# Second attention of a two-layer decoder: 384 equal slots, values in two blocks a group, transfers by four heads, norm rows on ScalarE

## The reference

```python
h = layernorm(x)                                   # over 256 columns
q, k, v from h @ W_kqv + b_kqv                     # 16 heads of 16
att = q @ k.T / sqrt(16) + slope * (j - i)         # j > i masked
x = x + (softmax(att) @ v) @ W_proj + b_proj
```

## Time and profile before

| | us |
|---|---|
| median of 3 runs | 2440.0 |
| the runs | 2440.0, 2426.59, 2440.98 |
| the profiled execution, span from first to last instruction | 2440.0 |
| the stage's first projection to its last addition | 808 to 1405 |
| first key score to last | 844.3 to 1390.6 |

### The profile page before, as it was taken

One profiled execution on the slowest core, in us unless ns is written; L12 is line 12 of the kernel. 1 busy time (PEld: TensorE's weight loads), 2 busy tenths in 40 slices (PEclk: granted clock), 3 DMA queues, 4 the chain that ended last, 5 costly groups with the idle time before them and its releaser, 6 DMA issues. The chain is left out here.

```text
span 2440.0 us, 41800 instructions
## 1 busy us (share of the span) xinstructions
PE 2194.9 (90%) x13788; PEld 1746.8 (72%) x13789; DVE 1186.6 (49%) x3470; ACT 961.3 (39%) x1878; POOL 641.1 (26%) x821
## 2 busy tenths in 40 slices
PE   6997888779999688888889879988999999999998
PEld 4664455568999445555555457778899999999998
DVE  4553788755334456666665345535322222222245
ACT  2222455333444344444444413320255555555411
POOL 1112667744401233333332211105400000000063
PEclk9997999889999789998999889989999999999999
DMA  9930000123222424442333010054211111111033
GB/s 321 386 109 1 1 1 33 46 72 117 70 69 84 97 54 88 88 88 49 83 80 70 2 56 4 3 193 148 88 31 34 34 34 34 32 32 34 26 110 101
DMA packets 151007, 183.45 MB, mean 75 GB/s; under 512 B 25490, under 2 KB 119250, under 8 KB 150738
## 3 DMA queue, kind: packets, MB, share of 16 engines
q1 hardware_dynamic: 136962, 146.51, 21.0%
q0 software_dynamic: 12288, 33.57, 4.4%
q10 hardware_dynamic: 1616, 1.57, 0.2%
HBM read 73.34 MB, written 74.19 MB: 60 GB/s over the span
## 5 line engine op out<-in xcount | busy, mean ns | idle before, releaser
L2462 ACT ACTIVATE a_prob<-a_st_ps 128x512 f32<-128x512 f32 (+1 forms) x384 | 197.6, 523 | 302.5 <-PE a_st_ps L2341 300.3
L2539 DVE CUSTOM_DVE_ANT_0 a_s_ps<-a_s_ps,a_causal 128x512 f32<-128x512 f32 (+3 forms) x512 | 241.0, 515 | 124.2 <-PE a_s_ps L2324 123.5
L1983 PE MATMUL e_up_ps<-e_xT,e_ring 128*128 128x128 f32 x2272 | 276.7, 275 | 0.0
L1983 PEld LDWEIGHTS e_up_ps<-e_xT,e_ring 128*128 128x128 f32 x2272 | 270.7, 192 | 3.7
L1935 POOL DMA_INDIRECT e_wgu<-slots_y,slot x64 | 61.2, 957 | 620.1 <-DMA slots_y<-e_y 575.6
L2013 ACT ACTIVATE e_ring<-e_wgu 128x512 f32 (+2 forms) x355 | 180.9, 531 | 75.6 <-PE e_up_ps L1983 73.9
L2324 PE MATMUL a_s_ps<-a_ks,rf_qs 68*128 68x512 f32 (+3 forms) x512 | 155.9, 373 | 60.7 <-DVE a_most L2539 47.5
L2018 ACT ACTIVATE e_hT<-e_up_ps 128x512 f32<-128x512 f32 x103 | 61.5, 597 | 371.9 <-PE e_y_ps L1993 364.4
L2341 PE MATMUL a_st_ps<-rf_qs,a_ks 128*128 128x512 f32 (+3 forms) x512 | 186.4, 415 | 15.7 <-DMA rf_qs<-a_m_lo 12.5
L2254 POOL TENSOR_SCALAR_AFFINE_SELECT a_prob<-a_prob 128x256 f32<-128x256 f32 x256 | 101.8, 423 | 367.2 <-ACT a_prob L2462 367.0
L1993 PE MATMUL e_y_ps<-e_wd,e_hT 128*128 x852 | 195.7, 379 | 0.0
(11 more groups left out here) (465 smaller groups left out, 4021.5 us busy)
## 6 DMA issues: line engine op xcount, KB each, us to landing
slots_x<-zero_row SPq DMA_DIRECT2D x4, 8448.0 KB, 50.6
e_xin<-slots_x SPq DMA_DIRECT2D x142, 128.0 KB, 2.0
rf_qs<-late_w SPq DMA_DIRECT2D x64, 256.0 KB, 5.8
a_ks<-late_w SPq DMA_DIRECT2D x64, 256.0 KB, 6.4
slots_x<-e_y SPq DMA_DIRECT2D x71, 128.0 KB, 1.7
slots_y<-e_y SPq DMA_DIRECT2D x71, 128.0 KB, 1.7
e_wgu<-in_L_ffn_wg SPq DMA_DIRECT2D x8, 688.0 KB, 9.7
e_wgu<-in_L_ffn_wu SPq DMA_DIRECT2D x8, 688.0 KB, 10.9
```

What stands on the lines that cost most here:

```text
L1983: last = pe.matmul(up_ps[:, j, bank, (first + n) * P:(first + n + 1) * P], weights, xT[:, j, k * P:(k + 1) * P], start=k == 0, stop=k == K ...
L2462: act.activation(prob[:, gr % 2, u // 3, (u % 3) * BANK:(u % 3) * BANK + cols], st_ps[:, u % 2, 0:cols], ACT.Exp).then_inc(exp_done, 1)
L2539: last = dve.tensor_tensor_reduce(s_ps[:, u % 2, off:off + cols], s_ps[:, u % 2, off:off + cols], causal[:, S - cols:], 1.0, -3.0e38, ALU. ...
```

## The change

The query score of unit s is computed in slot s - 18 (`LEAD`), one in each of 384 slots, beside one key score. Values stand in two blocks a group (key tile 0 in slot 3, tiles 1 to 3 in slot 5). `low_maxima` stands in slot 8 of a group, as `high_maxima`, and `turn_maxima` in slot 7. The transfers that spread queries and keys are made by four heads (a group) and wait for that group's exponentials alone; the weights' columns are ordered so that a group lies on 64 partitions. The norm's rows are written by ACT (`scalar_rows`, scale and offset) instead of DVE. In the first sequence the value projections come ahead of the third and fourth query and key projection, the transfers of the keys of groups 0 and 1 are issued by ACT, and DVE combines and takes statistics before the first maximum. All side work has new slots.

```diff
-    SCORES_AT = (1, 2, 1, 2, 1, 2, 1, 2, 0, 0, 0, 0)
-    TURN_AT, OUTPUTS_AT, KEPT_AT, TURN_OUTPUTS_AT = 9, 3, 7, 11
+    SEQ = G * UNITS
+    SLOTS = B * SEQ
+    LEAD = UNITS + 6
+    OUTPUTS_AT = {3: (0,), 5: (1, 2, 3)}
+    TURN_MAXIMA_AT, HIGH_AT, LOW_AT, KEPT_AT, TURN_OUTPUTS_AT, NORMALISE_AT = 7, 8, 8, 9, 11, 1
+    VALUES_AT, KEEP_VALUES_AT = {0: 0, 1: 1, 2: 2, 4: 3}, {6: 0, 7: 1}
+    ROWS_AT, TURN_ROWS_AT, KEEP_ROWS_AT = {1: 0, 3: 1, 4: 2, 5: 3}, 9, 9
+    QK_AT, HIGH_QK_AT, LOW_QK_AT = {11: 0, 13: 1, 34: 2, 37: 3}, {12: 0, 14: 1, 35: 2, 38: 3}, {13: 0, 15: 1, 36: 2, 39: 3}
+    TURN_HEADS_AT, KEEP_HEADS_AT, PROJECT_AT, ADD_AT = 20, 20, {22: 0, 24: 1, 26: 2, 29: 3}, {26: 0, 31: 1}
+    COMBINE_AT, STATS_AT, WHOLE_STATS_AT = {17: 0, 18: 1, 28: 2, 29: 3}, {33: 0, 34: 1, 35: 2, 37: 3}, 40
...
+        def spread_part(eng, b, gr, part, which):
+            n = gr % (P // GP) * GP
+            dst, src = ((qs, (hi, lo)[part % 2][n:n + GP, 0]), (ks, (hi, lo)[part // 2][n:n + GP, 1]))[which]
+            eng.dma_start(dst[part:PARTS:4, gr * GH:(gr + 1) * GH, :].bitcast(F32), src.bitcast(F32)).then_inc(spread[gr], 16)
...
+            def spread_group(b, gr):
+                sp.wait_ge(qk_lo, 4 * b + 2 * (gr // 2) + 2)
+                after(sp, exp_done, UNITS * (G * (b - 1) + gr + 1))
                 for part in range(4):
...
+            sp.wait_ge(qk_lo, 2)
+            for gr in range(2):
+                for part in range(4):
+                    spread_part(sp, 0, gr, part, 0)
+            place_maxima(0)
+            spread_group(0, 2)
+            spread_group(0, 3)
+            for b in range(B):
+                if b:
+                    spread_group(b, 3)
                 for gr in range(G):
+                    if G * b + gr + 1 < B * G:
+                        place_maxima(G * b + gr + 1)
+                    if b + 1 < B and gr < G - 1:
+                        spread_group(b + 1, gr)
...
+            for slot in range(SLOTS):
+                n, u = slot // UNITS, slot % UNITS
+                b, at = slot // SEQ, slot % SEQ
+                if slot + LEAD < SLOTS:
+                    score_by_query(slot + LEAD)
+                if u in OUTPUTS_AT and n:
+                    for t in OUTPUTS_AT[u]:
+                        outputs(n - 1, t)
+                if u == TURN_MAXIMA_AT and n + 1 < B * G:
+                    turn_maxima(n + 1)
+                if b and at in VALUES_AT:
+                    project_v(b, VALUES_AT[at])
+                if b + 1 < B:
+                    if at == TURN_ROWS_AT:
+                        norm.tensor(b + 1, free=[(v_kept, 2 * b + 2)])
+                    if at in QK_AT:
+                        project_qk(b + 1, QK_AT[at])
+                if b:
+                    if at == TURN_HEADS_AT:
+                        turn_heads(b - 1)
+                    if at in PROJECT_AT:
+                        project_out(b - 1, PROJECT_AT[at])
+                if u == TURN_OUTPUTS_AT and n:
+                    turn_outputs(n - 1)
+                score_by_key(slot)
...
+            act.wait_ge(qk_lo, 2)
+            for gr in range(2):
+                for part in range(4):
+                    spread_part(act, 0, gr, part, 1)
+            for i in range(2):
+                keep_values(0, i)
             act.wait_ge(front.slopes_placed, SLOPES)
...
+                exponential(slot)
+                if u == HIGH_AT and n + 1 < B * G:
+                    high_maxima(n + 1)
...
+                    if at in ROWS_AT:
+                        norm.scalar_rows(b + 1, tiles=(ROWS_AT[at],))
...
-                    if gr == 0 and nxt is not None:
-                        norm.vector_rows(nxt)
...
+                if slot + LEAD < SLOTS:
+                    maximum(slot + LEAD)
+                if u == LOW_AT and n + 1 < B * G:
+                    low_maxima(n + 1)
+                if u == NORMALISE_AT and n >= 2:
+                    normalise(n - 2)
```

More of the change, by code:

```diff
@@ L2190, in l1_attention @@
         w_done, x_done = sem("w_done"), sem("x_done")
-        spread = [sem(f"spread{i}") for i in range(KT)]
+        spread = [sem(f"spread{i}") for i in range(G)]
         m_placed = [sem(f"m_placed{i}") for i in range(G)]
@@ L2516, in _ @@
-            over_sequences_ahead(body)
-            keep_outputs(B - 1, G - 1)
+            high_maxima(0)
+            for slot in range(SLOTS):
+                n, u = slot // UNITS, slot % UNITS
+                b, at = slot // SEQ, slot % SEQ
+                exponential(slot)
+                if u == HIGH_AT and n + 1 < B * G:
+                    high_maxima(n + 1)
+                if b and at in KEEP_VALUES_AT:
+                    keep_values(b, KEEP_VALUES_AT[at])
+                if b + 1 < B:
+                    if at in ROWS_AT:
+                        norm.scalar_rows(b + 1, tiles=(ROWS_AT[at],))
+                    if at == KEEP_ROWS_AT:
+                        norm.scalar(b + 1, free=[(v_done, 2 * b + 2)])
+                    if at in HIGH_QK_AT:
+                        high_qk(b + 1, HIGH_QK_AT[at])
+                if b and at == KEEP_HEADS_AT:
+                    keep_heads(b - 1)
+                if u == KEPT_AT and n:
+                    keep_outputs(n - 1)
@@ L2534, in maxima @@
                     after(dve, m_turned, n - 1)
-                for u in units:
-                    wait_apart(dve, s_done, UNITS * n + u + 1, (ready, READY))
-                    for t, off in Q_UNITS[u % 3]:
-                        cols = (t + 1) * P
-                        last = dve.tensor_tensor_reduce(s_ps[:, u % 2, off:off + cols], s_ps[:, u % 2, off:off + cols], causal[:, S - cols:], 1.0,
-                                                        -3.0e38, ALU.add, ALU.max, most[:, gr % 2, u // 3, t:t + 1])
-                    last.then_inc(max_done, 1)
@@ L2543, in low_maxima @@
-            def low_maxima(b, gr):
-                n = b * G + gr
+                wait_apart(dve, s_done, s + 1, (ready, READY))
+                for t, off in Q_UNITS[u % 3]:
+                    cols = (t + 1) * P
+                    last = dve.tensor_tensor_reduce(s_ps[:, u % 2, off:off + cols], s_ps[:, u % 2, off:off + cols], causal[:, S - cols:], 1.0,
+                                                    -3.0e38, ALU.add, ALU.max, most[:, n % 2, u // 3, t:t + 1])
+                last.then_inc(max_done, 1)
@@ L2628, in _ @@
+            normalise(B * G - 2)
+            normalise(B * G - 1)
             for i in range(2):
```

324 lines of the change are left out of this document (125 added, 199 removed).

## The result

The changed kernel took 2353.17 us (median of 4 runs, 2350.1 to 2356.31) where the kernel before took 2439.68 on the same chip: ratio 0.9666, interval 0.964 to 0.9692, so 3.3% or 86.5 us faster. The forecast was 2406 and the range ended at 2372: the sign was right and the size was not. A second measurement, beside the experiments, gave 2354.87 against 2437.4 us, 0.9659 (0.9625 to 0.9694), 82.5 us.

The account below looks back on a forecast made before the run. PE's streaming, switches and waits were taken as the bound: 43.6 + 10.3 + 7.5 = 61.4 us a clean sequence, 4.4 less. Times 7.5 that is 33 us, plus 2 for the start, off 2440.0: forecast 2406 us, range 2372 to 2441.

Parts of the forecast that it names:

- streaming: PE's matmul passes in a clean sequence of the second attention: 43.6 us, foretold to stay.
- Switches, 10.3 us after: PE's changes of operand shape in a clean sequence: 10.2 us before, 1.9 and 0.6 more, 2.4 less, so 10.3 us.
- Four blocks of values, 2.4 us a sequence: Values on PE: 8 blocks a sequence instead of 16, 8 x 0.30 = 2.4 us less of switches.
- Waits, 7.5 us after: Real waits in a clean sequence, slot by slot: 7.5 us instead of 12.0, bounds 2 and 17 us.
- low maxima: Slot 8: DVE waits some 0.6 us for ACT's high part, then is late with the next unit: 4 x 0.5 = 2.0 us.
- ACT's rows: Norm rows added on ACT, 2.4 us a sequence, delay a key unit here and there: 1.0 us of waits.
- Half clock is taken as unchanged: PE's clock in the stage's steady part, mean 0.92 before: no gain counted; leaving 0.88 to 0.96 would show the forecast wrong.
- rival B: Much faster: waits near 3 us a sequence and the clock holds, 2368 us; chance 0.13.
- The start: Stage's start: value projections fill PE's hole, first key score near 847 (+2.5 us); sum -2 us, bounds -8 and +8.
- maxima from about 829: Stage's start: after combination and statistics, DVE takes maxima from about 829 at 0.93 us each, 18 units before the first key score.
- A: No change that can be told: waits only move, waits 10 us and switches 12 a sequence, 2438 us; chance 0.22.
- C: Slower: DVE and ACT set the slot, waits 17 us a sequence, start 8 us later, 2486 us; chance 0.08.

Follow-up runs that it names:

- e2: The changed kernel with values in four blocks a group again (slots 3, 4, 5 and 6, one key tile each): 2425.98 us, ratio 0.9667.
- e6: The changed kernel with the low part of the maxima on DVE in slot 10 instead of slot 8: 2381.05 us, ratio 0.9762.
- e3: The changed kernel with the norm's rows written by DVE again instead of ACT, in the same slots: 2424.19 us, ratio 0.9662.
- e1: The changed kernel with query scores in bursts again (1, 2, 1, 2, 1, 2, 1, 2, four times none a group): 2492.33 us, ratio 0.993.
- e9: The changed kernel with three pairs and three empty slots a group (2, 1, 1, 1, 2, 1, 1, 1, 2, 0, 0, 0): 2385.81 us, ratio 0.98.
- e10: The changed kernel with four pairs of query scores in slots 5, 7, 9 and 11, none in slots 0 to 3, 21 ahead: 2502.69 us, 0.9974.
- e5: The changed kernel with query scores in bursts, values in four blocks and norm rows on DVE, all taken back together: 2428.79 us, ratio 0.9969.
- b2: The kernel before with query scores as 2, 1, 1, 1, 2, 1, 1, 1, 2 and three times none: 2401.66 us, ratio 0.9865.
- e7: The changed kernel with ACT keeping the values before it issues the eight key transfers in the first sequence: 2351.23 us, ratio 0.964.
- b1: The kernel before with values in two blocks a group (slots 3 and 5): 2454.88 us, ratio 1.009.

## Why the prediction was wrong in size

The bound was read right: the stage is one of waits and switches on PE, with two thirds of it streaming. Of the three parts of a clean sequence, streaming was left at 43.6 us and is so, by the same accounting: PE's counts hold (342 and 343). The excess over it was 22.2 and fell to 13.3, not to the 17.8 of the prediction. The terms that failed follow. As estimates from the figures below, the switches account for some 25 us of the 52 between the foretold gain of 35 and the measured 86.5, the clock for 15, and the waits for 9.

**Switches, 10.3 us after: mis-sized from one row.** "A 512-column key score is followed by a query score after 0.34 instead of 0.21 (0.12 lost)". That row was not a plain one. The key score at 1024.79 came behind values, its own weight load had not gone ahead of it, and this is the row that the prediction didn't look at:

```profile
1024.79 0.19 PEld L2341 LDWEIGHTS a_st_ps<-rf_qs,a_ks 128*128 128x128 f32 x1 [0.84 <-issue]
```

Load and matmul start together, at 1024.79. So the 0.34 hold an exposed load of some 0.1 us. It is a cost of the block of values in front, to be paid once a block, and it was multiplied by 48 slots, of which only 16 have a 512-column key score. After the change that changeover takes 0.23 to 0.25, 0.02 of it lost, in most of the places where the key score stands directly behind a query score (54 of 96 in the six middle sequences; in the others a wait is added); behind the 24 that follow values it is still 0.33 to 0.34. Loads also stay exposed, by 0.06 to 0.12 us, behind short passes and behind waits. I put the true switches after at about 7 us, an estimate from such pairs of starts. In the kernel before no 512-column key score that a query score follows stands directly behind another query score (of 72 in the six middle sequences 48 stand behind values and 24 behind projections and transposes). So more rows of the same kind would have said 0.34 again; the 256-column pair at 988.97, shown above, would have told. How the 22.2 us of before divide into switches and waits was not taken again this way. The Trainium skill (TensorEngine Tiling, Key Properties) ties the drain to a change of tiling mode; the prediction weighed it and set it aside for this row, and the rule was right: 0.02 us lost between the two kinds of score, and 0.11 to 0.15 us lost on the way into values and out of them.

**Four blocks of values, 2.4 us a sequence:** 1.0 in e2, and not measurable in the time. Part of a switch lies where PE would wait anyway: with four blocks PE's waits for maxima are 7.9 us in the six middle sequences instead of 12.2.

**Waits, 7.5 us after: about 1 us too many,** the rest of the 13.3 being some 6.3. For maxima 4.4 us came as foretold (4), for the columns 1.1 (1.0). But the low maxima wait 1.0 us once a sequence, not four times 0.5 with a late unit behind each, and e6 shows that even this costs PE nothing; ACT's rows have no price in the trace of e3. That the rhythm of pairs and empty slots costs the time, as the prediction said, is shown by e1: 66 of 84 us. That it costs by the wait for maxima alone is not: in e1 that wait is half of PE's added idle time, and in e9 little of it.

**"Half clock is taken as unchanged": some 15 us wrong.** The clock of the steady part went from 0.92 to 0.96 (0.95 in the second profile), still inside the band of 0.88 to 0.96 that I had named as the sign. With pairs back it was 0.93 (e1), with late pairs 0.87 (e10). But it doesn't follow the pairs strictly: e5 has four pairs, a clock of 0.99 in its six middle sequences, as the changed kernel, and takes 400.4 us for them instead of 344.6. So the equal slots win without the clock, and what the clock gives comes on top. The Trainium skill (TensorE: Matmul & The Clock Gate, What's actually happening) ties half clock to an idle engine; the traces agree in part: with 36.3 us of waits for maxima in six sequences the clock was 0.95, with 48.7 it was 0.90, with 12.2 it was 0.99, but with 28.2 it was 1.00 (b2). That rule spoke for rival B, which I held at 0.13.

**The start,** −2 us foretold, came as +5.1 to the first exponential. Of that 2.4 lie before the stage, at its first instruction, so +2.7 are its own, against the +2.5 foretold for the first key score; the first and last sequence gave back some 7. A small gain in all, inside its bounds. The step "maxima from about 829" was wrong: the first query score came 22.6 us behind the stage's first matmul where it had been 21.2, since ACT issued its eight transfers, in 8.72 us, before it kept the values (e7 turns the two around and has 19.1).

**The rivals.** A (waits only move) and C (DVE sets the slot) are out: DVE is busy 43.25 of 56.86 us, 76%, and waits 12.1 us for PE. B (waits 3 us each sequence, clock holds, 2368) had the nearer number and half of its reasons: the clock held largely, the waits fell to about 6, not to 3, and what makes up for it is the switches that never were. That its number came near is in part luck.

**What stays open.** Why the fourth pair costs as much as three. The patterns differ in place too, and no run separates the two. That pairs cost in a second place too is shown by e10; how its 0.87 clock comes about is not. Nor is it shown how much of what e1 and e9 lose would stay if the side work on ACT were laid out for pairs.

## What to carry to other kernels

With two buffers between a producer and a consumer of equal rates, issue one unit in each slot: here pairs now and none later cost 2.6 us in every 14.4, and the empty slots gave nothing back. Before a switch is priced from a row, see that neither of its two instructions stands behind another switch (load and matmul starting together is the sign), and take it from pairs in the order that the new kernel will have. A change that shortens waits on PE may give back half-clock time as well, some 15 us here, though b2 had the clock at 1.00 with long waits left. And waits of two versions are compared over equal work, not over equal time.

## What the runs showed that I had not expected

Issues of transfers became slow when many stood close together: SP and ACT took 8.05 and 8.72 us for eight each in the start (the timeline above), about 1.0 us an issue, where SP's median is 597 ns over the stage. That two queues at once are the cause isn't shown. SP's first three took 0.58 to 0.64 us beside ACT's, and only then did they take 0.87 to 1.40; in the kernel before SP alone took 0.70 to 1.08 us for its fifth to eighth. The issue times (ns, min/median/max) of the changed kernel are

```profile
L2208 SPq DMA_DIRECT2D rf_qs<-late_w x128: 537/597/1399, 818.2 to 1255.0; - x128
L2208 ACTq DMA_DIRECT2D a_ks<-late_w x8: 662/925/1680, 818.2 to 825.7; - x8
```

and the 128 KB of one landed in 2.4 us at the median (ACT's eight in the start in 5.5), where 256 KB took 5.8. And a block of three key tiles, which I took for a saving anywhere, made the kernel before 0.9% slower (b1).
